# Two stages of a decoder kernel: conv attention with two mix banks, latent attention with two value parts

## The chip, the cores and the metric

One core of a Trainium2 chip runs the kernel. The metric is the device time of one execution in microseconds, as the median over runs.

## The reference

The model is a decoder with two layers. The residual stream x has 4 batches of 1024 rows of 256 numbers. The kernel computes six stages, a to f; the change touches two of them, the conv attention (stage d) and the latent attention (stage e). Cut to these:

```python
def _L1_attn_ref(query, Wq, bq, Wk, bk, Wv, bv, Wo, bo, conv_w, conv_b):   # H = 16 heads of 16
    Q = (query @ Wq.T + bq)...; K = ...; V = ...
    scores = jnp.einsum('bhqd,bhkd->bhqk', Q, K) / np.sqrt(dh)
    # a convolution of width 3 along the keys, over the heads as channels
    x = lax.conv_general_dilated(x, conv_w, window_strides=(1,), padding=[(KS // 2, KS // 2)], ...)
    weights = jax.nn.softmax(x + conv_b, axis=-1)
    out = jnp.einsum('bhqk,bhkd->bqhd', weights, V).reshape(b, s, e)
    return out @ Wo.T + bo

def _L1_xattn_ref(x, latents, mask, ...):                                   # 4 heads of 64
    xn = layernorm(x, ln_x_g, ln_x_b)            # x: the context, 77 rows
    ln = layernorm(latents, ln_l_g, ln_l_b)      # latents: the stream, 1024 rows
    q = ln @ W_q
    kv = jnp.concatenate([xn @ W_kv, ln @ W_kv], axis=1)
    qn = rmsnorm(q, q_gamma) * SCALE; kn = rmsnorm(k, k_gamma)
    sim = jnp.einsum('bhid,bhjd->bhij', qn, kn)  # masked
    attn = jax.nn.softmax(sim, axis=-1)
    out = jnp.einsum('bhij,bhjd->bhid', attn, v)
    return out @ W_out + b_out

x = x + _L1_attn_ref(_layernorm(x), ...)
x = x + _L1_xattn_ref(ctx_1024, _layernorm(x), mask_BxS2_bk0, ...)
```

## The kernel before

Every engine has a program of its own, an instruction list in a fixed order written out by loops in the source; semaphores (`wait_ge`, `then_inc`) tie them together. SP issues the DMAs.

**Conv attention** (`stage_conv_attention`, the span's 860 to 2678 us). The work is 512 units: 4 batches times 16 heads times 8 tiles of 128 query rows. `u` counts them, `b = u // 128`, `at = u % 128`. The score banks are three buffers of two PSUM banks each (banks 0 to 5); banks 6 and 7 are `mix_bank` and `back_bank`. For each unit:
- TensorE, `scores(u)` (L2066): 12 matmuls of 512 columns. It waits for `probs_low` of unit u-3, which frees the buffer.
- VectorE, `maximum(u)` (L2331, L2335), then, in the same turn of its loop, `low_probs(u-1)` (L2340).
- ScalarE, `exps(u)` (L2222), in six of eight units a tap of the key convolution (L2211) or a key half (L2217), then `high_probs(u)` (L2229).
- SP, a DMA transpose of the two halves into `probsT` (L1996). `probsT` has two buffers, one for even and one for odd groups of four units.

For each group of four units: TensorE `mix_values` (L2082: 16 matmuls, each on 32 columns of the array, four side by side), ScalarE `move_mixT` (L2238) from `mix_bank` to `group_mixT`, TensorE `turn_back` (L2092: 4 transposes into `back_bank`), VectorE `normalize` (L2350, L2352, L2355) into `mix`. With `MIX_LAG = 5` the mix of group g stands behind the scores of unit 4g+7, the copy ahead of exps(4g+8), the turn-back behind scores(4g+9), the normalisation at the end of VectorE's turn 4g+10.

The work between batches is spread over the units as "fills", all through `back_bank`: transposes and output products of the batch before (`TURN_FILL`, `OUT_FILL`, units 3 to 16, L2103, L2115), and for the next batch the norm's transposes (`NORM_FILL`, 36 to 48, L2123), query and key columns (`Q_FILL`, `K_FILL`, 52 to 80, L2131) and values (`V_FILL`, 84 to 96, L2138), each at every fourth unit. A fill waits for the normalisation that last read `back_bank`, and the next `turn_back` waits until the fill has been copied out.

**Latent attention** (`stage_latent_attention`, 2678 to 3362 us). First the context's 77 rows are normed and projected (L2598 to L2730). Then for each of four batches: a projection stretch of 14 steps (norm transposes, queries and keys with an RMS norm, their transposes, values), and a score loop of 32 units (4 heads times 8 tiles), taken in pairs. TensorE's order in the loop is scores(2p), scores(2p+1), `project` (L2882), `mix_values` (L2864 to L2873) of earlier pairs. `scores(u)` waits for the exp of unit u-2. The probabilities go exp (L3030), high half (L3037) on ScalarE, low half (L2936) on GpSimd, DMA transpose by SP (L2788) into `probsT`; `halves` and `probs` have three buffers. A value is kept as three bf16 parts: high (ScalarE L3012), left (VectorE L3096), middle (ScalarE L3017), low (GpSimd L2927). A mix multiplies high and middle in one set of 18 matmuls of 128 columns (L2864, L2866), and low in a second set of 18 of 64 columns (L2870, L2873). The norm of the next batch runs inside the loop: `stats` at units 8 to 11, `aggregate` 11 to 14, `rstd_step` on GpSimd 15 to 21, `apply` (L3140) 22 to 29, `add_bias` on GpSimd from 23 on.

## Time and profile before

| | us |
|---|---|
| median of the runs | 3918.76 |
| lowest, highest | 3916.62, 3923.54 |
| the profiled execution | 3912.23 |
| its span | 3910.5 |
| TensorE busy in the span | 3369.3 (86%) |
| VectorE busy | 2928.5 (75%) |
| ScalarE busy | 2601.1 (67%) |
| GpSimd busy | 1826.9 (47%) |
| conv attention, mean DMA share | 0.87 |

Busy times are of one profiled execution. A unit's place in time is read from the timeline, by the start of its first score matmul (two matmuls are merged in one row, "x2"). A row's first two numbers are start and duration in microseconds, those in square brackets the idle time of the engine ahead of it and what ended it.

### The profile page before, as it was taken

The numbers are of one execution on the slowest core, as the hardware profiler recorded it, in microseconds if no ns is written. First come the engines' busy times: TensorE is split into PE (matmuls) and PEld (weight loads), VectorE is DVE, ScalarE is ACT, GpSimd is POOL, SyncE is SP. The second block draws the span as 40 slices with busy tenths as digits, with TensorE's granted clock in tenths as the row PEclk, the third lists the DMA queues.
The fourth block names the chain that finished last, engine by engine and source line by source line (L and its number), as shares of the span: only waits on it lengthen the run. The fifth ranks groups of instructions, "written<-read, shape, count | busy, mean of one in ns | idle before, by whom it ended". The sixth has DMA issues, their size and how long they took to land. (4 is left out here: it accounts for less than half of the span.)

```text
span 3910.5 us, 61085 instructions
## 1 busy us (share of the span) xinstructions
PE 3369.3 (86%) x20113; PEld 2602.9 (67%) x20113; DVE 2928.5 (75%) x5833; ACT 2601.1 (67%) x3897; POOL 1826.9 (47%) x1129
## 2 busy tenths in 40 slices
PE   6867724269999999999999999995889899799999
PEld 4645521147777777777777777773667667699999
DVE  4568789779888888888888889984676666474347
ACT  2334444558888888898888989982667667354443
POOL 0034410016656566565665656642767576360015
PEclk9989956589999999999999999997999999799999
DMA  1047800038889888888888889891749467743224
GB/s 51 0 87 129 147 22 1 1 110 157 151 147 154 147 151 151 146 156 143 154 146 151 155 149 162 162 165 36 124 85 174 80 121 140 204 149 95 76 83 146
DMA packets 1571351, 470.02 MB, mean 120 GB/s; under 512 B 1507174, under 2 KB 1565159, under 8 KB 1569767
## 3 DMA queue, kind: packets, MB, share of 16 engines
q1 hardware_dynamic: 1564903, 449.40, 60.7%
q0 software_dynamic: 6144, 16.79, 1.3%
q8 instruction: 164, 2.69, 0.3%
q14 instruction: 140, 1.15, 0.1%
HBM read 49.00 MB, written 39.58 MB: 23 GB/s over the span
## 5 line engine op out<-in xcount | busy, mean ns | idle before, releaser
L2331 DVE TENSOR_REDUCE d_neg_max<-psum 128x1 f32<-128x1024 f32 x512 | 624.6, 1220 | 161.9 <-PE psum L2066 160.7
L2066 PE MATMUL psum<-d_KH,d_QH 128*128 128x512 f32 x2048 | 685.3, 416 | 25.5 <-DVE d_halves L2340 21.0
L2222 ACT ACTIVATE psum<-psum,d_bias 128x1024 f32<-128x1024 f32 x512 | 558.2, 1090 | 213.9 <-DVE d_bias L2335 203.5
L2340 DVE SCALAR_TENSOR_TENSOR d_halves<-psum,d_halves 128x1024 f16<-128x1024 f32 x512 | 624.3, 1219 | 32.3 <-ACT d_halves L2229 27.7
L2066 PE MATMUL psum<-d_KL,d_QH 128*128 128x512 f32 x2048 | 638.1, 393 | 0.0
L2066 PE MATMUL psum<-d_KH,d_QL 128*128 128x512 f32 x2048 | 636.7, 392 | 0.0
L2022 POOL TENSOR_TENSOR d_KC<-d_KC,d_tap_of 128x1024 f32<-128x1024 f32 x126 | 302.1, 2397 | 536.6 <-ACT d_tap_of L2211 536.6
L2229 ACT ACTIVATE d_halves<-psum 128x1024 f16<-128x1024 f32 x512 | 521.6, 1019 | 3.5
L2066 PEld LDWEIGHTS psum<-d_KH,d_QH 128*128 128x128 f32 x2048 | 356.9, 188 | 173.1 <-issue 68.4
L2066 PEld LDWEIGHTS psum<-d_KL,d_QH 128*128 128x128 f32 x2048 | 384.9, 188 | 87.7
L2066 PEld LDWEIGHTS psum<-d_KH,d_QL 128*128 128x128 f32 x2048 | 384.9, 188 | 87.0
L2029 POOL TENSOR_TENSOR d_KL<-d_KC,d_KH 128x1024 fp32r<-128x1024 f32 x128 | 308.1, 2407 | 112.7 <-ACT d_KH L2217 112.7
L2936 POOL TENSOR_TENSOR e_halves<-e_probs,e_halves 128x1102 f16<-128x1102 f32 x128 | 292.2, 2283 | 122.9 <-ACT e_halves L3037 121.5
L2018 POOL TENSOR_TENSOR d_KC<-d_KC,d_tap_of 128x1024 f32<-128x1024 f32 x126 | 306.8, 2435 | 26.2 <-ACT d_tap_of L2211 17.9
L2211 ACT ACTIVATE d_tap_of<-d_K,d_taps 128x1024 f32<-128x1024 f32 x252 | 288.8, 1146 | 0.0
L3030 ACT ACTIVATE e_probs<-psum,e_neg_max 128x1102 f32<-128x1102 f32 x128 | 150.3, 1174 | 92.9 <-DVE e_neg_max L3109 92.8
L3105 DVE TENSOR_REDUCE e_own_neg_max<-psum 128x1 f32<-128x1102 f32 x128 | 167.1, 1305 | 4.4
L3494 POOL DMA_INDIRECT f_tile<-f_expert_out,f_slots x64 | 60.8, 950 | 231.7 <-DMA f_expert_out<-f_tile 183.8
L3781 DVE TENSOR_TENSOR f_hT_low<-psum,f_hT_high 128x384 fp32r<-128x384 f32 x135 | 75.3, 558 | 117.4 <-ACT f_hT_high L3657 117.2
L3653 ACT ACTIVATE f_silu<-psum 128x352 f32<-128x352 f32 x135 | 62.8, 466 | 145.7 <-PE psum L3543 143.0
L3037 ACT ACTIVATE e_halves<-e_probs 128x1102 f16<-128x1102 f32 x128 | 143.7, 1122 | 23.6 <-DMA e_probsT<-e_halves 20.4
L3657 ACT ACTIVATE f_hT_high<-psum 128x384 fp32r<-128x384 f32 x135 | 66.4, 492 | 137.1 <-PE psum L3563 137.0
(526 smaller groups left out, 7577.7 us busy)
## 6 DMA issues: line engine op xcount, KB each, us to landing
f_weights_raw<-in_L_ffn_packed_dram SPq DMA_DIRECT2D x10, 1088.0 KB, 16.1
f_tile<-expert_rows SPq DMA_DIRECT2D x71, 128.0 KB, 2.2
f_expert_out<-f_tile SPq DMA_DIRECT2D x71, 128.0 KB, 1.7
d_probsT<-d_halves SPq DMA_TRANSPOSE x512, 4.3
f_tile<-f_kept_rows SPq DMA_DIRECT2D x64, 128.0 KB, 2.2
expert_rows<-d_group_mixT SPq DMA_DIRECT2D x7, 1024.0 KB, 11.5
residual_stream<-in_x_dram SPq DMA_DIRECT2D x4, 1024.0 KB, 9.5
f_kept_rows<-residual_stream SPq DMA_DIRECT2D x4, 1024.0 KB, 8.5
```

Of the source, the lines that this page charges most:

```text
L2018: g.tensor_tensor(KC[:, ch, :], KC[:, ch, :], tap_of[:, ch, :], ALU.add)\
L2022: g.tensor_tensor(KC[:, ch, :], KC[:, ch, :], tap_of[:, ch, :], ALU.add)\
L2029: g.tensor_tensor(KL[hh % 2][:, ch, :], KC[:, ch, :], KH[hh % 2][:, ch, :].bitcast(F32), ALU.subtract).then_inc(key_low.sem, 1)
L2066: last = t.matmul(scores_at(u)[:, cols], q_part[:, ch, j * P:(j + 1) * P], k_part[hh % 2][:, ch, cols], start=k == 0, stop=k == 5)
L2211: a.activation(tap_of[:, ch, :], K[b % 2][:, ch, k:S + k], ACT.Copy, scale=taps[:, ch, 3 * h + k:3 * h + k + 1]).then_inc(tapped.sem, 1)
L2222: a.activation(scores_at(u), scores_at(u), ACT.Exp, bias=bias[u % 2][:, 0:1], accum_out=sums[u // 4 % 4][:, u % 4, :]).then_inc(probs_read ...
L2229: a.activation(halves[u % 4][:, 0, :], scores_at(u), ACT.Copy, scale=LIFT)\
L2331: v.tensor_reduce(neg_max[u % 2][:], scores_at(u), AXIS.X, ALU.max, negate=True)\
L2340: v.scalar_tensor_tensor(halves[u % 4][:, 1, :], scores_at(u), LIFT, halves[u % 4][:, 0, :], ALU.mult, ALU.subtract).then_inc(probs_low.se ...
L2936: g.tensor_tensor(halves[i % 3][:, 1, 0:W], probs[i % 3][:], halves[i % 3][:, 0, 0:W], ALU.subtract)\
L3030: a.activation(probs[g % 3][:], scores_at(g), ACT.Exp, bias=neg_max[g % 2][:, 0:1], accum_out=sums[p % 2][:, i:i + 1]).then_inc(probs_read ...
L3105: v.tensor_reduce(own_neg_max[g % 2][:], scores_at(u), AXIS.X, ALU.max, negate=True)\
```

## The change

In the conv attention the mixes of two groups (an even one and the following odd one) stand together behind the scores of unit 8p+11. Even groups use PSUM bank 6, odd groups bank 7, for mix and turn-back both; a mix from group 2 on waits for the normalisation of the group two before. The copies stand ahead of exps 8p+12 (even) and 8p+14 (odd), the turn-backs behind scores 8p+13 and 8p+15, the normalisations in VectorE's turns 8p+14 and 8p+16. The fills get new units and take the bank that `fill_bank` names; turn and out fills alternate by `banks[k // 2]`.

In the latent attention a value is kept as two f16 parts, scaled by a power of two that is worked out from the weights at the stage's start (squares on ScalarE, one matmul, small steps on VectorE, a power on GpSimd); `wo` is scaled back once. The second set of matmuls, the middle copy and GpSimd's low part are gone. The norm's steps stand at other units, and `apply` is another instruction.

```diff
-        mix_bank = PS[:, 6 * BANK:7 * BANK]
-        back_bank = PS[:, 7 * BANK:8 * BANK]
+        banks = [PS[:, 6 * BANK:7 * BANK], PS[:, 7 * BANK:8 * BANK]]
+
+        def fill_bank(at):
+            return banks[0 if at % 8 in (7, 0) else 1]
...
-        TURN_FILL = {3: 0, 4: 1, 7: 2, 8: 3}
-        OUT_FILL = {11: 0, 12: 1, 15: 2, 16: 3}
-        NORM_FILL = {36 + 4 * k: k for k in range(4)}
-        Q_FILL = {52 + 4 * k: k for k in range(4)}
-        K_FILL = {68 + 4 * k: k for k in range(4)}
-        V_FILL = {84 + 4 * k: k for k in range(4)}
-        TAIL = 18
+        PAIRS = GROUPS * B // 2
+        TURN_FILL = {7: 0, 8: 1, 9: 2, 10: 3}
+        OUT_FILL = {15: 0, 16: 1, 17: 2, 18: 3}
+        NORM_FILL = {39: 0, 41: 1, 47: 2, 49: 3}
+        Q_FILL = {55: 0, 57: 1, 63: 2, 65: 3}
+        K_FILL = {71: 0, 73: 1, 79: 2, 81: 3}
+        V_FILL = {87: 0, 89: 1, 95: 2, 97: 3}
+        TAIL = 20
+        MIX_AT, EVEN_MOVED, EVEN_BACK, EVEN_NORM, ODD_MOVED, ODD_BACK, ODD_NORM = 11, 12, 13, 14, 14, 15, 16
...
-                    t.wait_ge(mixT_moved.sem, mixT_moved.at(group))
+                    if group >= 2:
+                        t.wait_ge(normalized.sem, normalized.at(group - 1))
...
+                    pair = pair_at(u, MIX_AT)
+                    if pair is not None:
+                        wait_for_fill(b, at - 3 if at - 3 in FILLS else at - 4)
+                        mix_values(2 * pair)
+                        wait_for_fill(b, at - 1 if at - 1 in FILLS else at - 2)
+                        mix_values(2 * pair + 1)
+                    pair = pair_at(u, EVEN_BACK)
+                    if pair is not None:
+                        turn_back(2 * pair)
+                    pair = pair_at(u, ODD_BACK)
+                    if pair is not None:
+                        turn_back(2 * pair + 1)
+                    if at % 8 in (7, 0):
+                        groups = 2 * ((u - EVEN_BACK) // 8) + 1
+                    else:
+                        groups = 2 * ((u - ODD_BACK) // 8) + 2
...
-        V = sb("V", [P, TB, H, PARTS * HD], BF16)
+        V = sb("V", [P, TB, H, 2 * HD], F16)
...
                     for k in range(TB):
                         for part in range(2):
-                            t.matmul(mix_bank, V[:, k, h, 0:2 * HD], moving(part, k), start=k + part == 0, stop=False)
+                            t.matmul(mix_bank, V[:, k, h, :], moving(part, k), start=k + part == 0, stop=False)
                     for part in range(2):
-                        t.matmul(mix_bank, ctx_values[:, b, h, 0:2 * HD], moving(part, TB)[0:Z, :], start=False,
-                                 stop=False)
-                    for k in range(TB):
-                        for part in range(2):
-                            t.matmul(mix_bank[part * HD:(part + 1) * HD, :], V[:, k, h, 2 * HD:3 * HD],
-                                     moving(part, k), start=False, stop=False)
-                    for part in range(2):
-                        last = t.matmul(mix_bank[part * HD:(part + 1) * HD, :], ctx_values[:, b, h, 2 * HD:3 * HD],
-                                        moving(part, TB)[0:Z, :], start=False, stop=True)
+                        last = t.matmul(mix_bank, ctx_values[:, b, h, :], moving(part, TB)[0:Z, :], start=False,
+                                        stop=part == 1)
...
-                def values_low(b, j):
-                    g.wait_ge(v_middle.sem, v_middle.at(TB * b + j + 1))
-                    g.tensor_tensor(V[:, j, :, 2 * HD:3 * HD], left[j % 2][:], V[:, j, :, HD:2 * HD], ALU.subtract)\
-                        .then_inc(v_low.sem, 1)
...
-                        if b + 1 < B and 15 <= u < 22:
-                            rstd_step(b + 1, u - 15)
-                        if b + 1 < B and 23 <= u < 23 + TB:
-                            add_bias(TB * (b + 1) + u - 23)
+                        if b + 1 < B and 9 <= u < 16:
+                            rstd_step(b + 1, u - 9)
+                        if b + 1 < B and 22 <= u < 22 + TB:
+                            add_bias(TB * (b + 1) + u - 22)
...
-                def value_left(b, j):
+                def value_low(b, j):
                     v.wait_ge(v_high.sem, v_high.at(TB * b + j + 1))
-                    v.wait_ge(v_low.sem, v_low.at(TB * b + j - 1))
-                    v.tensor_tensor(left[j % 2][:], bank(j % 2)[:, 0:D].rearrange("p (h e) -> p h e", h=H),
-                                    V[:, j, :, 0:HD], ALU.subtract).then_inc(v_left.sem, 1)
+                    v.scalar_tensor_tensor(V[:, j, :, HD:2 * HD],
+                                           bank(j % 2)[:, 0:D].rearrange("p (h e) -> p h e", h=H), v_scale[:, 0:1],
+                                           V[:, j, :, 0:HD], ALU.mult, ALU.subtract).then_inc(v_low.sem, 1)
...
-                    v.tensor_scalar(n.xn[:, tile, :], X[:, TB * b + tile, :], n.mv[:, tile, 0:1],
-                                    n.rstd[:, tile:tile + 1], ALU.subtract, ALU.mult).then_inc(n.normed.sem, 1)
+                    v.scalar_tensor_tensor(n.xn[:, tile, :], X[:, TB * b + tile, :], n.mv[:, tile, 0:1],
+                                           n.rstd[:, tile:tile + 1].to_broadcast([P, D]), ALU.subtract, ALU.mult)\
+                        .then_inc(n.normed.sem, 1)
...
-                        if b + 1 < B and 8 <= u < 12:
-                            stats(b + 1, 2 * u - 16)
-                            stats(b + 1, 2 * u - 15)
-                        if b + 1 < B and 11 <= u < 15:
-                            aggregate(b + 1, 2 * u - 22)
-                            aggregate(b + 1, 2 * u - 21)
+                        if b + 1 < B and 3 <= u < 7:
+                            stats(b + 1, 2 * u - 6)
+                            stats(b + 1, 2 * u - 5)
+                        if b + 1 < B and 6 <= u < 10:
+                            aggregate(b + 1, 2 * u - 12)
+                            aggregate(b + 1, 2 * u - 11)
```

## Rows read from the trace of the kernel before

**Rows 1.** Windows: stretch, its us, busy us of each engine, PEclk, DMA share, GB/s

```profile
875.00:2645.00 1770.00, 1730.35 (x9043) 1286.35 (x9041) 1547.72 (x2067) 1555.14 (x2106) 1072.07 (x524) 1.00 0.87 152
3265.00:3340.00 75.00, 73.80 (x584) 60.04 (x583) 47.66 (x101) 56.18 (x81) 52.84 (x24) 1.00 1.03 176
```

**Rows 2.** Timeline of TensorE, conv stage, from unit 152 to unit 160

```profile
1401.26 0.74 PE L2066 MATMUL psum<-d_KH,d_QH 128*128 128x512 f32 x2
...
1406.90 0.60 PE L2092 MATMUL psum<-ident,d_group_mixT 128*128 128x128 f32 x4
1407.26 0.71 PE L2066 MATMUL psum<-d_KH,d_QH 128*128 128x512 f32 x2
...
1427.38 0.73 PE L2066 MATMUL psum<-d_KH,d_QH 128*128 128x512 f32 x2
```

**Rows 3.** Timeline of TensorE around one mix

```profile
1453.55 0.62 PE L2066 MATMUL psum<-d_KL,d_QH 128*128 128x512 f32 x2
1454.01 0.63 PE L2066 MATMUL psum<-d_KH,d_QL 128*128 128x512 f32 x2
1454.56 1.05 PE L2082 MATMUL psum<-d_probsT,d_V 128*32 128x512 f16 x16
1455.54 0.74 PE L2066 MATMUL psum<-d_KH,d_QH 128*128 128x512 f32 x2
1456.12 0.63 PE L2066 MATMUL psum<-d_KL,d_QH 128*128 128x512 f32 x2
```

**Rows 4.** Timeline of VectorE and ScalarE, unit 152 and the next maximum

```profile
1404.34 1.23 DVE L2331 TENSOR_REDUCE d_neg_max<-psum 128x1 f32<-128x1024 f32 x1 [0.42 <-PE psum L2066]
...
1405.91 1.09 ACT L2222 ACTIVATE psum<-psum,d_bias 128x1024 f32<-128x1024 f32 x1 [0.34 <-DVE d_bias L2335]
...
1407.10 1.22 DVE L2331 TENSOR_REDUCE d_neg_max<-psum 128x1 f32<-128x1024 f32 x1
1408.06 1.01 ACT L2229 ACTIVATE d_halves<-psum 128x1024 f16<-128x1024 f32 x1
...
1409.11 1.23 DVE L2340 SCALAR_TENSOR_TENSOR d_halves<-psum,d_halves 128x1024 f16<-128x1024 f32 x1 [0.47 <-ACT d_halves L2229]
```

**Rows 5.** Timeline, a normalisation and the turn fill that waits for it

```profile
1324.80 0.68 DVE L2350 TENSOR_REDUCE d_group_sum<-psum 128x64 f32<-128x512 f32 x1
...
1325.94 0.42 PEld L2103 LDWEIGHTS psum<-ident,d_mix 128*128 128x128 f32 x4 [0.49 <-DVE d_mix L2355]
```

**Rows 6.** Timeline of TensorE, a column fill and one octet, unit 181 to 189

```profile
1499.64 1.88 PE L2131 MATMUL psum<-d_ln_xT,d_wq 128*128 128x512 f32 x4
1500.95 1.03 PE L2066 MATMUL psum<-d_KH,d_QH 128*128 128x512 f32 x2
...
1529.69 1.03 PE L2066 MATMUL psum<-d_KH,d_QH 128*128 128x512 f32 x2
```

**Rows 7.** Timeline of TensorE, latent stage, one mix and the scores behind it

```profile
3288.44 1.91 PE L2864 MATMUL psum<-e_probsT,e_V 128*128 128x256 f16 x16
...
3290.50 1.06 PE L2870 MATMUL psum<-e_probsT,e_V 128*64 128x256 f16 x16
...
3291.61 0.50 PE L2845 MATMUL psum<-e_KH,e_QS 128*128 128x512 f32 x1
```

**Rows 8.** Timeline of TensorE, the scores seven pairs later

```profile
3337.95 0.50 PE L2845 MATMUL psum<-e_KH,e_QS 128*128 128x512 f32 x1
```

**Rows 9.** Page, DMA issues: operation, count, median us to landing

```profile
e_probsT<-e_halves SPq DMA_TRANSPOSE x128, 4.8
```

**Rows 10.** Page, groups: busy us, mean ns, idle before

```profile
L2936 POOL TENSOR_TENSOR e_halves<-e_probs,e_halves 128x1102 f16<-128x1102 f32 x128 | 292.2, 2283 | 122.9 <-ACT e_halves L3037 121.5
L3037 ACT ACTIVATE e_halves<-e_probs 128x1102 f16<-128x1102 f32 x128 | 143.7, 1122 | 23.6 <-DMA e_probsT<-e_halves 20.4
```

**Rows 11.** By line: duration ns min/median/max, first and last start

```profile
L3140 DVE TENSOR_SCALAR e_ln_xn<-residual_stream,e_ln_mean_var,e_ln_rstd x24: 406/946/2032, 2836.8 to 3180.8; 128x256 f32<-128x256 f32 x24
...
L2368 DVE TENSOR_TENSOR d_QL<-d_ln_xn,d_QH x32: 411/418/2496, 859.7 to 2223.3; 128x256 fp32r<-128x256 f32 x32
```

More of the change, by code:

```diff
@@ L2081, in mix_values @@
                             part, tile = lane % 2, k + lane // 2
-                            last = t.matmul(mix_bank[lane * 32:(lane + 1) * 32, :], V[:, side, tile, h, :],
+                            last = t.matmul(banks[group % 2][lane * 32:(lane + 1) * 32, :], V[:, side, tile, h, :],
                                             probsT[group % 2][:, part * TB + tile, :, :]
@@ L2087, in turn_back @@
                 def turn_back(group):
-                    if group:
-                        t.wait_ge(normalized.sem, normalized.at(group))
                     t.wait_ge(mixT_moved.sem, mixT_moved.at(group + 1))
                     for k in range(4):
-                        last = t.transpose(back_bank[:, k * P:(k + 1) * P], group_mixT[:, k * P:(k + 1) * P],
+                        last = t.transpose(banks[group % 2][:, k * P:(k + 1) * P], group_mixT[:, k * P:(k + 1) * P],
                                            core.ident[:])
@@ L2100, in turn_mix @@
                         t.wait_ge(mixT_ready.sem, mixT_ready.at(4 * b + k))
+                    bank = banks[k // 2]
                     for i in range(2):
                         for ch in range(DC):
-                            last = t.transpose(back_bank[:, (ch * 2 + i) * P:(ch * 2 + i + 1) * P],
+                            last = t.transpose(bank[:, (ch * 2 + i) * P:(ch * 2 + i + 1) * P],
                                                mix[:, 2 * k + i, ch * P:(ch + 1) * P], core.ident[:])
@@ L2292, in _ @@
                     b, at, hh, j = u // U, u % U, u // TB, u % TB
-                    if u >= MIX_LAG + 3 and (u - MIX_LAG - 3) % 4 == 0 and (u - MIX_LAG - 3) // 4 < GROUPS * B:
-                        move_mixT((u - MIX_LAG - 3) // 4)
+                    pair = pair_at(u, EVEN_MOVED)
+                    if pair is not None:
+                        move_mixT(2 * pair)
+                    pair = pair_at(u, ODD_MOVED)
+                    if pair is not None:
+                        move_mixT(2 * pair + 1)
                     if u < ALL:
@@ L2520, in stage_latent_attention @@
     KB = WP // P
-    PARTS = 3
+    V_REACH = float(1 << 15)
     TILES = TB * B
@@ L2687, in _ @@
                 def _(t):
+                    t.wait_ge(v_squares_done.sem, v_squares_done.at(3))
+                    t.matmul(PS[:, 6 * BANK:6 * BANK + 3], core.ones[:], v_squares[:], start=True, stop=True)\
+                        .then_inc(v_totalled.sem, 1)
                     t.wait_ge(ctx_vec.sem, ctx_vec.at(3 * B))
```

184 lines of the change are left out of this document (110 added, 74 removed).

## The prediction

> **Which views, in which order.** First the busy table of stretches [rows 1], to be read by stage: a change in one stage is worth what that stage's last wait gives. In the conv stage TensorE is busy 1730 of 1770 us, VectorE 1548 and ScalarE 1555: three engines near their limit. In the latent stage's score loop TensorE is busy 73.8 of 75 us, and the DMA engines show a share of 1.03. Neither stage has an engine whose relief alone shortens it much. Then the timelines, to see which wait ends last.
>
> **Conv stage, a stretch without fills.** Eight units take 26.1 us, from 1401.26 to 1427.38 [rows 2]. I name the units of an octet 0 to 7. TensorE's own work in it: a score unit is 12 matmuls of 0.23 (two of them step by 0.46, [rows 3]), so 2.75. The first unit behind a mix is 2.87, because the next pair of matmuls comes after 0.58 and not 0.46. A mix is 0.98, entered 0.09 late, at 1454.56 and not 1454.47. A turn-back is 0.36 [rows 2]. For eight units: 22.2 + 2 x 1.07 + 2 x 0.36 = 25.0. So 1.1 us of every octet is waiting: scores(u) needs low_probs(u-3).
>
> One unit on the other engines [rows 4]: its maximum starts 2.96 to 3.08 after its scores do; exp follows 1.57 after the start of the maximum; the high half starts 2.15 after exp when a tap stands between and takes 1.01; the low half takes 1.23. VectorE's step from one maximum to the next is 2.76, and a normalisation adds 1.0 (one starts at 1324.80 and the TensorE that waits for it is freed at 1325.94, 1.1 later [rows 5]). So VectorE needs 8 x 2.76 + 2 x 1.0 = 24.1.
>
> Walking the old order by hand with these durations (mixes behind units 3 and 7, copies before exp of 0 and 4, turn-backs behind 1 and 5, normalisations in 2 and 6) settles at 26.1 in the second octet: the row's value. That is why I trust the walk to some tenths.
>
> **The new order, same walk.** Two mixes stand behind unit 3. TensorE saves one exit and one entry: 0.12 + 0.09 + about 0.1 = 0.3 per octet, 64 octets, 20 us if TensorE sets the pace. But the burst is 0.1 + 0.98 + 0.86 = 1.93, and VectorE sits idle 1.4 us before unit 4's maximum. From the start of unit 3's scores to unit 6's maximum TensorE leads: 2.75 + 1.93 + 2.87 + 2.75 + 0.36 + 2.96 = 13.6. From there VectorE leads until the low half of the next unit 0, which unit 3 needs: four steps of 2.76, the two normalisations (now in iterations 6 and 0, so both inside this stretch) 2.0, and 0.2 of waiting for ScalarE: 13.2. Sum 26.8, against 26.1: +0.75 per octet. Some 30 of the 64 octets are without fills: **+23 us** (bounds 0 and +40).
>
> Beside the first rule of this walk: the Trainium skill (TensorEngine Tiling (Array Packing), Key Properties) says that changing the tiling mode drains TensorE. By that rule alone, fewer changes of mode mean a shorter stage, which is the rival 'Drained less' below. The trace agrees that a change costs: 0.09 at the entry [rows 3].
>
> **Octets with fills.** In the octets with query, key and value columns TensorE really is the bound: 28.74 us [rows 6], 25.0 + 2 x 1.31 for the columns + 2 x 0.4 by which the scores behind them are longer = 28.4. There 0.3 comes off. But a fill now stands one unit behind the normalisation that frees its bank (iteration 6 for the fill behind unit 7, iteration 0 for that behind unit 1); before it was two. The old turn_mix(0) stands one unit behind too, and there TensorE waits 0.49 even with a mix of 0.98 in between [rows 5]. A fill has no mix in between. By the walk: VectorE ends the normalisation 3.9 after unit 6's maximum starts, TensorE arrives 0.95 earlier; at the second fill 1.2 earlier. So +2.15 of waiting, less 0.3 and less the 0.2 of old slack: +1.7. There are 6 such octets in each of three batches: 18 x 1.7 = **+30 us** (bounds +8 and +45). In the 6 octets with norm transposes the wait that leaves (turn_back had to wait for the fill's copy in the one shared bank) is as large as the new one: 0. The turn and out fills save about 2 us, since two banks alternate; the tail has both turn-backs behind the last transposes, +2. SP's transposes of an even group now wait for a mix that ends some 4 us later; they catch up, since at a share of 0.87 one is 3.0 us of DMA time in a unit of 3.45 [rows 1], and the high half that reuses the buffer comes 4 us later still: 0. If that cover were gone, ScalarE would wait for the transposes once per octet, and behind it exp of the next unit. The wait for the normalisation that mix_values now carries is met by an operation of the octet before: 0.
>
> Conv stage: +23 + 30 + 0 = **+53 us**.
>
> **Latent stage.** A pair of units: 18 matmuls of 128 columns from 3288.44, 18 of 64 columns from 3290.50, the next scores at 3291.61 [rows 7]. The second set goes: 1.11 + 0.1 for its entry = 1.2 us of TensorE per pair. The mean pair takes (3337.95 - 3291.61)/7 = 6.62 [rows 7, 8]. TensorE would then need some 5.3: it stops being the bound, and the whole 1.2 can't be had. What is late next:
> - the score loop: scores(u) need exp(u-2). My estimate from the loop's unit times, scores 1.35, mask and maximum 1.85, exp, high half and next exp 3.6, with the overlap of two units, gives 5.5 per pair.
> - the DMA queue: at share 1.03 a transpose costs 1.03 x 3.31 = 3.4 us of 16 engines. I take 1.15 as the share it can reach: 2.95 each, 5.9 per pair.
> - the three buffers of halves: high half 1.12, low half 2.28 [rows 10], transpose 4.8 to landing [rows 9], some 0.2 between: 8.4 us, and nearer 9 with two transposes in flight. Three units per 9 us is 6.0 per pair.
>
> I take 6.0: 0.6 per pair on 44 pairs = 26 us. In the last four pairs of the first three batches the apply of the next norm holds VectorE: 0.95 us median, 0.41 at best [rows 11]. The change writes it as scalar_tensor_tensor with two SBUF tensors. That form's nearest row is the conv stage's QL, also two SBUF tensors: 0.41 at best, 2.50 where a GpSimd operation runs [rows 11]. So the new apply waits for GpSimd as the old one, and these 12 pairs gain 0.2: 2 us. The first mix of a batch stands on the path: 1.1 x 4 = 4. In the stretch between batches the last three mixes and the value steps lose 3.5 each time: 10. (Two of the three mixes are on the path there, 2.4; the rest is that a value bank comes free after two steps and not behind ScalarE's middle copy and GpSimd's low part, which go too.) The tail: 3. At the stage's start three squares on ScalarE, one matmul, seven small VectorE steps and one pow on GpSimd are new, and the pow stands ahead of the next norm's chain; one split of the context's values goes from VectorE's path. I bound this between -1 and +3 and take 0. The statistics (units 3 to 6) and the rstd steps on GpSimd (9 to 15, between its low halves) move ahead; VectorE's are hidden where it waits for the first mix, GpSimd's are the same work in another place: 0, and 2 us if the two pows now delay a transpose that was not late before. Sum **-46 us** (bounds -20 and -75).
>
> The Trainium skill (SBUF — State Buffer, Who interferes with whom) says that a VectorE instruction with two SBUF inputs contends with a GpSimd instruction that reads SBUF. It speaks against the new apply, and the 2.50 us row agrees.
>
> **Sum.** +53 - 46 = +7 us. The profiled execution took 3912.23 (span 3910.5), 6.5 below the median of the runs, 3918.76; so 3919 in the profile's terms, and **3926** as a median. 0.2% of this kernel, 8 us, is about what a measurement can tell from no change.
>
> **Rivals.**
> - *Drained less* (0.2). TensorE is the bound all over the conv stage, normalisations come in time, and the stage gives the 20 us of the 64 saved entries and exits. For it: 97.8% busy [rows 1]. Against it: the 1.1 us per octet of waits. 3918.8 - 20 - 46 = 3853.
> - *Latent at its compute limit* (0.22). The DMA queue carries 5.5 per pair: 44 x 1.15 = 51 rather than 26: 3901 to 3907. For it: DMA share is not shown to be a limit. Against it: 1.03 already. This is the case on the other side of mine; it decides from a share of 3.41 x 2 / 5.5 = 1.24 up.
> - *Held by the transposes* (0.24). The pair stays near 6.4, latency growing as the queue fills: 10 us from the pairs and -29 in all; with the bound of +30 for the no-fill octets: 3943 to 3955.
> - *Forecast* (0.34): 3911 to 3941.
> - That the third part of the values is not removed is excluded by the diff.
>
> **Chances.** Below 3911: all of the first, most of the second (0.16), 0.04 of the forecast: 0.40. Within 8 us: 0.17. Above: 0.43. Cases of both signs are likely, the forecast's own range is 3911 to 3941. The range for 8 in 10 runs from 3862, which leaves out half of the first rival, to 3956.
>
> **What would show it.** Right: fill-free octets near 26.8, the scores of units 1 and 3 waiting for d_halves; column octets near 30.4, with a wait for d_mix of about 1 us before L2131's matmuls; pairs near 6.0 with DMA share about 1.15; the apply still near 1 us. Wrong: octets at 25.8 and 28.4, or pairs at 5.5.

## The result, and the profile of the changed kernel

The changed kernel takes 3987.69 us in the median (3983.34 to 3992.21), the kernel before 3921.15 (3916.62 to 3927.30) beside it: a ratio of 1.0167, 95% interval 1.0148 to 1.0185. Forecast was 3926, with a range up to 3956. The profiled executions have spans of 3985.2 and 3910.5. Read by stage, from the first instruction of one stage to the first of the next:

| stage | before | after | difference | forecast |
|---|---|---|---|---|
| ahead of the conv attention | 830.0 | 833.2 | +3 | 0 |
| conv attention | 1848.2 | 1947.6 | **+99** | +53 |
| latent attention | 688.7 | 661.6 | **-27** | -46 |
| behind it | 543.6 | 542.8 | -1 | 0 |

Both stages moved the way that was forecast, and both missed its size to the slower side. A stage's length differs between profiles of one and the same code: the latent stage of before took 685.3 to 693.1 us in eight profiles (before and seven experiments), that of after 661.6 to 666.1 in three. The windows of the two stages (stretch, its us, busy us of each engine, PEclk, DMA share, GB/s) answer to [rows 1]:

```profile
885.00:2745.00 1860.00, 1730.16 (x9028) 1297.90 (x9028) 1555.52 (x2059) 1549.05 (x2099) 1061.74 (x522) 1.00 0.81 145
3345.00:3420.00 75.00, 65.17 (x398) 52.94 (x396) 50.79 (x107) 58.55 (x85) 54.24 (x24) 0.98 1.03 179
```

In the conv stage the engines do the same work (TensorE 1730 busy in both) in 1860 us and not 1770: TensorE fell from 97.8% to 93% busy. What came in is waiting. In the latent stage TensorE has 65 us of work in 75 where it had 74, and the DMA share is 1.03 as before.

What TensorE waited for in the conv stage (engine, line, releaser: us in total, times, longest), first before:

```profile
PE psum L2066 <- DVE d_halves L2340: 21.0, 38, 2.2
PE psum L2092 <- ACT d_ln_xT L2245: 5.7, 12, 1.0
PE psum L2115 <- DVE d_mix L2355: 2.3, 6, 0.6
```

and after:

```profile
PE psum L2073 <- DVE d_halves L2368: 56.2, 75, 2.4
PE psum L2139 <- DVE d_mix L2383: 27.1, 24, 1.4
PE psum L2131 <- DVE d_mix L2383: 13.8, 12, 1.3
PE psum L2146 <- DVE d_mix L2383: 13.0, 12, 1.1
PE psum L2123 <- DVE d_mix L2383: 9.4, 6, 2.0
```

63 us of waits of fills for a normalisation (`d_mix`), and 35 us more of scores waiting for the low half three units back. A fill-free octet of the last batch, TensorE's timeline (start, us), from one burst of two mixes to the next:

```profile
2593.45 1.91 PE L2090 MATMUL psum<-d_probsT,d_V 128*32 128x512 f16 x32
...
2611.17 0.73 PE L2073 MATMUL psum<-d_KH,d_QH 128*128 128x512 f32 x2 [0.71 <-DVE d_halves L2368]
2617.33 0.73 PE L2073 MATMUL psum<-d_KH,d_QH 128*128 128x512 f32 x2 [0.38 <-DVE d_halves L2368]
2620.28 1.91 PE L2090 MATMUL psum<-d_probsT,d_V 128*32 128x512 f16 x32
```

2620.28 - 2593.45 = 26.83. The walk gave 26.8, with the scores of units 1 and 3 waiting for d_halves: so it is. Its two stretches, read from the starts and ends in the timeline, are 13.8 (from unit 3's scores to unit 6's maximum; forecast 13.6) and 13.0 (from there to the end of the low half of the next unit 0; forecast 13.2). An octet with query columns:

```profile
1534.63 1.91 PE L2090 MATMUL psum<-d_probsT,d_V 128*32 128x512 f16 x32
...
1549.93 1.98 PE L2139 MATMUL psum<-d_ln_xT,d_wq 128*128 128x512 f32 x4 [1.29 <-DVE d_mix L2383]
...
1558.44 1.98 PE L2139 MATMUL psum<-d_ln_xT,d_wq 128*128 128x512 f32 x4 [1.01 <-DVE d_mix L2383]
...
1565.86 1.91 PE L2090 MATMUL psum<-d_probsT,d_V 128*32 128x512 f16 x32
```

31.2 us (28.74 before [rows 6]; forecast 30.4). VectorE and GpSimd around the first of the two waits:

```profile
1548.10 0.68 DVE L2378 TENSOR_REDUCE d_group_sum<-psum 128x64 f32<-128x512 f32 x1
1548.97 0.90 DVE L2383 TENSOR_TENSOR d_mix<-d_group_sum,d_inv_sum 128x64 f32<-128x64 f32 x1
```

```profile
1548.52 1.27 POOL L2054 TENSOR_TENSOR residual_stream<-residual_stream,d_bo 128x512 f32<-128x512 f32 x1
```

L2383 takes 0.22 to 0.24 alone; here 0.90, and it ends 0.08 behind GpSimd's addition. The same instruction of the same octets is as long in before (0.91), where two units lie between it and the fill. TensorE pays for that now, since it stands behind this normalisation.

The 63 whole octets of the stage, each from the start of unit 4's maximum to that of the next octet's, after less before, by what stands in them (sums over the batches, worked out from the starts of the 512 maxima in either timeline; an apply is the last step of a norm on one tile, a split takes the low part of the queries, both on VectorE):

| octets | count | difference, us | forecast |
|---|---|---|---|
| none of what follows | 27 | +21 | 27 x 0.75 = +20 |
| columns and values | 18 | +43.5 | +30 |
| applies of the next norm (units 28 to 36) | 3 | +7.0 | counted with the first row, +2.3 |
| splits of the next queries (units 124 to 132) | 3 | +6.0 | counted with the first row, +2.3 |
| norm transposes | 6 | +4.9 | 0 |
| turn and out fills | 6 | +14.2 | -2 |
| beginning and tail | | +3 | +2 |

Of the last row's 3 us, 2.2 lie ahead of the first maximum, where the profiles read 41.7 to 44.0 in no order of the kernels; the tail gives 0.8.

The latent stage: its four score loops take 393.3 us, from the first maximum of each to its last, before 412.9; the three gaps between loops 164.5 (170.0); from the last maximum to the next stage 23.5 (25.5); the beginning 80.3 (80.2). Mix and scores of a pair, to [rows 7]:

```profile
3374.31 1.91 PE L2937 MATMUL psum<-e_probsT,e_V 128*128 128x256 f16 x16
...
3376.19 0.48 PE L2920 MATMUL psum<-e_KH,e_QS 128*128 128x512 f32 x1
...
3380.58 1.91 PE L2937 MATMUL psum<-e_probsT,e_V 128*128 128x256 f16 x16 [0.21 <-issue]
...
3387.91 1.91 PE L2937 MATMUL psum<-e_probsT,e_V 128*128 128x256 f16 x16
```

1.88 from mix to scores where it was 3.17; pairs of 6.27 and 7.33. ScalarE's high half (page, groups) and the apply (by line: min/median/max ns), to [rows 10, 11]:

```profile
L3092 ACT ACTIVATE e_halves<-e_probs 128x1102 f16<-128x1102 f32 x128 | 143.6, 1122 | 44.3 <-DMA e_probsT<-e_halves 41.3
```

```profile
L3194 DVE SCALAR_TENSOR_TENSOR e_ln_xn<-residual_stream,e_ln_mean_var,e_ln_rstd x24: 481/1164/2398, 2932.6 to 3264.7; 128x256 f32<-128x256 f32 x24
```

The wait for transposes went from 20.4 to 41.3 us, and the new apply is slower than the old one (1164 against 946).

### The profile page after: what moved, and what is told of

Same layout as the page of the kernel before. It is cut to its first block and busy times, and to the rows that moved or that the text cites. A ratio compares the mean times of both kernels' runs of the same rounds, so it can differ in the third digit from the quotient of the medians.

```text
span 3985.2 us, 58619 instructions
## 1 busy us (share of the span) xinstructions
PE 3306.3 (83%) x18960; PEld 2565.5 (64%) x18963; DVE 2947.1 (74%) x5839; ACT 2592.4 (65%) x3871; POOL 1799.0 (45%) x1098
## 5 line engine op out<-in xcount | busy, mean ns | idle before, releaser
L2073 PEld LDWEIGHTS psum<-d_KH,d_QH 128*128 128x128 f32 x2048 | 365.0, 189 | 202.7 <-DVE d_halves L2368 74.7
L3092 ACT ACTIVATE e_halves<-e_probs 128x1102 f16<-128x1102 f32 x128 | 143.6, 1122 | 44.3 <-DMA e_probsT<-e_halves 41.3
```

Of the source, the lines that this page charges most:

```text
L2073: last = t.matmul(scores_at(u)[:, cols], q_part[:, ch, j * P:(j + 1) * P], k_part[hh % 2][:, ch, cols], start=k == 0, stop=k == 5)
```

## The experiments

Times are medians; each ratio is to the kernel before, run beside it. Line numbers in the rows are those of each run's own kernel.

**Each half alone.** e1 has the conv attention of after and the latent attention of before; e2 the other way round.

```diff
 e1:  stage_conv_attention of after, stage_latent_attention of before
 e2:  stage_conv_attention of before, stage_latent_attention of after
```

> The conv attention of after, the latent attention of before. In the profile of after the conv stage starts at 833 and the latent stage at 2781, 1948 us, against 830 to 2678, 1848 us, in before: +99. If the stages are independent this kernel is at 3921 + 99 = 4020, between 4012 and 4028, slower than after. If the conv change also shifts something in the latent stage (clock, queue of transposes), it is off this by more than 8 us.

> The conv attention of before, the latent attention of after. The latent stage of after takes 661.6 us to the first work of the next stage, before 688.7: -27. Independent stages: 3921 - 27 = 3894, between 3887 and 3901. The forecast's term was -46, which would be 3875.

e1: 4013.72, ratio 1.0232 (1.0214 to 1.0250). e2: 3903.21, ratio 0.9935 (0.9916 to 0.9954). In the profiles the conv stage takes 1944.5 in e1, the latent stage 666.1 in e2. 1.0232 x 0.9935 = 1.0165, the ratio of the whole change within its interval: the two halves don't meet. By the medians they are +91 and -20, by the ratios +91 and -25. e2 lies just above its expected 3887 to 3901.

**Fills one unit later.**

```diff
-        NORM_FILL = {39: 0, 41: 1, 47: 2, 49: 3}
+        NORM_FILL = {40: 0, 42: 1, 48: 2, 50: 3}
 (Q_FILL, K_FILL, V_FILL alike)
```

> e1 with the norm, query, key and value fills one unit later (behind units 0 and 2 of an octet, not 7 and 1). Theory 'the fill waits for the normalisation': TensorE's waits for d_mix ahead of L2131, L2139 and L2146 (54 us in after) go nearly to zero, of the 2.4 us that a column octet lost some 1.5 to 2 come back, and the stage is 25 to 40 us shorter than in e1. Rival 'the wait only moves': the paired mixes behind unit 3 now wait for the copy of the fill behind unit 2, by 1 to 2 us per octet, and the stage is within 10 us of e1. Rival 'the burst of two mixes is the cost': the octets stay at 31.

3972.33, ratio 1.0133 (1.0110 to 1.0155); the stage is 1903.7, 41 less than in e1. One octet with query columns and one with key columns:

```profile
1540.25 2.04 PE L2090 MATMUL psum<-d_probsT,d_V 128*32 128x512 f16 x32
1557.23 1.88 PE L2139 MATMUL psum<-d_ln_xT,d_wq 128*128 128x512 f32 x4
1564.62 1.98 PE L2139 MATMUL psum<-d_ln_xT,d_wq 128*128 128x512 f32 x4
1567.20 0.73 PE L2073 MATMUL psum<-d_KH,d_QH 128*128 128x512 f32 x2 [0.59 <-DVE d_halves L2368]
1570.16 2.06 PE L2090 MATMUL psum<-d_probsT,d_V 128*32 128x512 f16 x32
...
1598.96 1.91 PE L2090 MATMUL psum<-d_probsT,d_V 128*32 128x512 f16 x32
1615.80 1.88 PE L2139 MATMUL psum<-d_ln_xT,d_wk 128*128 128x512 f32 x4
1623.02 1.88 PE L2139 MATMUL psum<-d_ln_xT,d_wk 128*128 128x512 f32 x4
1627.60 1.91 PE L2090 MATMUL psum<-d_probsT,d_V 128*32 128x512 f16 x32
```

No fill waits for d_mix, and the mixes behind unit 3 don't wait for the copy either: the first theory holds, the two others fall. With key columns an octet is 28.64, and before it was 28.73: TensorE has no idle time in it, and the switches saved give 0.1, not 0.3. With query columns it is 29.91, 1.2 above before, and the scores wait for the low half (0.59). With values it is 29.75 to 29.79 in five octets and 28.64 in one, the octet from 92 to 100 of the first batch. VectorE copies queries and values and not keys, but the copies aren't the difference: that one octet has the same four copies of 0.41 as its neighbour from 84 to 92. What differs is the second normalisation. Here it is in the octet from 84 to 92 (29.77 us), VectorE and GpSimd, and then in that from 92 to 100:

```profile
1186.02 2.33 DVE L2383 TENSOR_TENSOR d_mix<-d_group_sum,d_inv_sum 128x64 f32<-128x64 f32 x1
```

```profile
1185.87 2.41 POOL L2029 TENSOR_TENSOR d_KC<-d_KC,d_tap_of 128x1024 f32<-128x1024 f32 x1 [4.02 <-ACT d_tap_of L2235]
```

```profile
1215.78 0.22 DVE L2383 TENSOR_TENSOR d_mix<-d_group_sum,d_inv_sum 128x64 f32<-128x64 f32 x1
```

Started 0.15 behind GpSimd's instruction it lasts until that one ends; in the octet of 28.64 it starts 0.14 ahead of it and takes 0.22. All six octets with queries have it at 1.98 to 2.34, none of those with keys has. Of the 43.5 us some 32 go with the fills' later place (the 18 octets of e3 against those of e1); the 12 that are left stand in the 11 octets with the held normalisation.

**Two banks without the pairing.** Banks alternate, but each group's mix, copy, turn-back and normalisation stand where before had them, and so do the fills.

```diff
-        MIX_AT, EVEN_MOVED, EVEN_BACK, EVEN_NORM, ODD_MOVED, ODD_BACK, ODD_NORM = 11, 12, 13, 14, 14, 15, 16
+        EVEN_MIX, EVEN_MOVED, EVEN_BACK, EVEN_NORM = 7, 8, 9, 10
+        ODD_MIX, ODD_MOVED, ODD_BACK, ODD_NORM = 11, 12, 13, 14
-            return banks[0 if at % 8 in (7, 0) else 1]
+            return banks[0 if at % 8 in (3, 4) else 1]
+ (fills at the units of before)
```

> The conv attention with two banks as in after, even groups in bank 6 and odd groups in bank 7, but the mixes not paired: mix, copy, turn-back and normalisation of each group stand where before had them, and so do the fills, each in the bank that has just been normalised. The latent attention of before. Theory 'pairing is the cost, not the two banks': fill-free octets at 26.0 (26.85 in after), column octets at 28.7, no wait for d_mix at the fills, and turn_back no longer waits for a fill's copy (7 us in before): 3905 to 3921 in all. Rival 'alternating banks itself costs' (group_mixT has still one buffer, the mix waits for the normalisation of the group two before): octets of 26.8 and over, 3940 and more.

3914.25, ratio 0.9970 (0.9954 to 0.9986), 99 us below e1. The mixes of a fill-free octet at the same place as above:

```profile
2589.29 1.05 PE L2091 MATMUL psum<-d_probsT,d_V 128*32 128x512 f16 x16
2593.50 0.74 PE L2074 MATMUL psum<-d_KH,d_QH 128*128 128x512 f32 x2 [0.21 <-DVE d_halves L2371]
2602.43 1.05 PE L2091 MATMUL psum<-d_probsT,d_V 128*32 128x512 f16 x16
2615.22 1.05 PE L2091 MATMUL psum<-d_probsT,d_V 128*32 128x512 f16 x16
```

25.93 and not 26.83; column octets are at 28.73. The pairing is the whole cost, the held instructions included: from the first maximum to the last, e4 is 1.8 us shorter than before. The second bank alone is worth a little: the octets with norm transposes are 27.0 and 26.9 (28.1 and 27.4 before), since turn_back no longer waits for the fill's copy.

**Output products spread.**

```diff
-        OUT_FILL = {15: 0, 16: 1, 17: 2, 18: 3}
+        OUT_FILL = {16: 0, 24: 1, 26: 2, 34: 3}
-        TAIL = 20
+        TAIL = 36
```

> e3 with the four output products of the batch before behind units 16, 24, 26 and 34 (in e3 15 to 18). In e3 the octet from unit 12 to 20 takes 37.2 (31.15 in before), with waits for d_mix of 1.1 and 1.98 ahead of L2123 and, in after, a granted clock of 0.66 behind the second. Theory 'these waits and the clock behind them': no wait for d_mix ahead of L2123, the octets from 12 to 36 together 26.3 + 37.2 + 29.2 = 92.7 in e3 become 83 to 87, so 18 to 28 us less than e3. Rival 'the products themselves': each octet gets 1.5 per product and the sum is within 1.5 us of e3's.

3968.07, ratio 1.0118 (1.0094 to 1.0141). The three octets from 12 to 36 take 89.3, 90.9 and 87.2 in the batches that have products, in e3 91.2, 92.8 and 91.0: 2 to 4 less, where I expected 6 to 10. No product waits for d_mix any more, but each adds its 1.54 to a paired octet in full (27.1 + 26.3 + 29.2 + 4 x 1.54 = 88.8): the rival was the larger half. What the waits cost in after shows here, TensorE's timeline, the normalisation that it waited for, and the windows:

```profile
1411.07 2.51 PE L2123 MATMUL psum<-d_wo,d_K 128*128 128x256 f32 x8 [1.98 <-DVE d_mix L2383]
1413.02 1.41 PE L2073 MATMUL psum<-d_KH,d_QH 128*128 128x512 f32 x2
```

```profile
1409.03 1.98 DVE L2383 TENSOR_TENSOR d_mix<-d_group_sum,d_inv_sum 128x64 f32<-128x64 f32 x1 [0.46 <-DVE d_inv_sum L2380]
```

```profile
1404.00:1409.00 5.00, 5.00 (x23) 3.93 (x21) 3.91 (x6) 2.80 (x4) 0.41 (x1) 1.00 0.60 113
1411.00:1416.00 5.00, 4.93 (x15) 4.00 (x16) 3.24 (x5) 3.16 (x4) 2.15 (x2) 0.66 0.01 3
```

L2383 takes 1.98 here (2.34 in the two later batches) and not 0.22, beside a GpSimd instruction of 2.34 that started at 1408.59: 1.76 of the 1.98 us of TensorE's second wait are this hold. TensorE stood for 1.98 us, and behind it the granted clock is 0.66: the lower of its two levels, 1.2 GHz, for (1 - 0.66)/0.5 = 0.68 of these 5 us. The same pair of scores, which takes 1.41 at 1413.02, took 0.82 at 1405.97, behind the product before.

**What an octet is made of.** e6 makes the burst shorter, e7 the normalisation; both are from e1 and leave work out.

```diff
 e6:
-                    for k in range(0, TB, 2):
+                    for k in range(0, TB // 2 if group % 2 else TB, 2):
 e7:
-                    v.tensor_reduce(group_sum[:], parts, AXIS.X, ALU.add)
+                    v.tensor_reduce(group_sum[:, 0:1, :], parts[:, 0:1, :, :], AXIS.X, ALU.add)
```

> e1 with half of the matmuls of the odd group's mix left out (8 of 16; the output of the conv attention is then not the reference's): the burst of two mixes is 0.43 us shorter, VectorE has the same work. Theory 'an octet is a stretch led by TensorE, the burst in it, and then a stretch led by VectorE': a fill-free octet falls from 26.85 by about 0.4. Rival 'VectorE or ScalarE alone sets the octet': it stays at 26.85.

> e1 with the sum of a normalisation over a quarter of its columns (the output of the conv attention is then not the reference's): VectorE saves about 0.4 in each of two normalisations per octet, TensorE has the same work. By the same theory a fill-free octet falls from 26.85 by about 0.8, to 26.0 to 26.1, and the wait for d_mix ahead of the column fills by 0.4 each, so that a column octet falls from 31.1 to about 30.3. Rival 'TensorE's burst is all of it': 26.85 stays.

3983.78 and 3964.20, one run each. Bursts in the same octet of e6, then of e7:

```profile
2592.66 1.48 PE L2091 MATMUL psum<-d_probsT,d_V 128*32 128x512 f16 x24
2619.07 1.48 PE L2091 MATMUL psum<-d_probsT,d_V 128*32 128x512 f16 x24
```

```profile
2592.30 1.91 PE L2090 MATMUL psum<-d_probsT,d_V 128*32 128x512 f16 x32
2615.37 0.74 PE L2073 MATMUL psum<-d_KH,d_QH 128*128 128x512 f32 x2 [0.17 <-DVE d_halves L2369]
2618.34 1.91 PE L2090 MATMUL psum<-d_probsT,d_V 128*32 128x512 f16 x32
```

26.41 and 26.04. 0.43 us off TensorE's burst gives 0.42, all of it in the first stretch (13.8 to 13.4). In e7 the second stretch goes from 13.0 to 12.2 and the first stays. VectorE's two sums are 0.8 shorter (0.68 to 0.28 each); the first L2383 of the octet, which GpSimd held for 0.76, is down to 0.22 besides, so VectorE has 1.33 less to do and the octet gives 0.79. A new wait of the low half for ScalarE (0.26) takes a part of the rest. No single engine sets this octet: it is a stretch led by TensorE followed by one led by VectorE, as in the walk. The column octets of e7 fell to 30.8 (queries, beside GpSimd's additions) and 29.75 (keys, values); I expected 30.3.

**VectorE's other work.** From e1, the applies of the conv stage's next norm in other turns.

```diff
-                    if b + 1 < B and 27 <= at < 27 + TB:
-                        apply(b + 1, at - 27)
+                    if b + 1 < B and at in (27, 35, 43, 44):
+                        (two applies)
```

> e1 with the eight applies of the conv stage's next norm not one in each of VectorE's turns 27 to 34 but two in each of the turns 27, 35, 43 and 44, where VectorE then waits for the scores behind the burst of two mixes. The octet from 28 to 36 is 29.24 in e1 (26.92 in before). Theory 'work of VectorE costs its whole time in the stretch that VectorE leads and little ahead of the burst's end': that octet falls to 26.9 to 27.3, and the next one (28.57), whose turn 43 is ahead of the burst's end and turn 44 behind it, rises by no more than 0.8. Rival 'the work itself has to be paid anywhere': the two octets together keep their 57.8.

4015.60, one run. The octet from 28 to 36 fell to 26.84 in all three batches (29.24, 32.00 and 29.26 in e1); six applies in turns 27, 35 and 43 cost nothing. The two in turn 44 cost 1.7 (the octet from 44 to 52: 30.3, before the move 28.56), where I allowed 0.8. VectorE, and GpSimd beside it:

```profile
1505.18 2.00 DVE L2452 TENSOR_SCALAR d_ln_xn<-residual_stream,d_ln_mean_var,d_ln_rstd 128x256 f32<-128x256 f32 x2
```

```profile
1504.32 2.39 POOL L2036 TENSOR_TENSOR d_KL<-d_KC,d_KH 128x1024 fp32r<-128x1024 f32 x1
```

Two applies of 0.4 each took 2.0: the first 1.68, until 0.15 behind the end of GpSimd's instruction, the second 0.40. The rival falls for six of the eight. Turn 44 lies in a third octet, which the expectation left out; the three together go from 86.4 to 85.7 only. The experiment doesn't part two causes: the six applies that cost nothing took 0.40 each, while in after those of turns 28 and 33 took 1.68 and 1.10 (0.60 and 0.60 in before), so a turn without room and a turn beside GpSimd's instruction are the same turns here. What a hold alone costs shows in the second batch of e1, where the apply of turn 30 took 2.62 and the octet 32.0 and not 29.25, and in the third batch of e4 (2.64, and 30.5 and not 26.9).

**The latent attention.** From here every kernel has the conv attention of e4.

> The conv attention of e4 and the latent attention of after. Apart they gave 3914 and 3903 against 3923. Independent: 3923 - 9 - 20 to -25 = 3889 to 3895, faster than before by 0.7 to 0.9%.

e8: 3886.39, ratio 0.9910 (0.9892 to 0.9927), faster than either kernel and 3 us below the expected 3889 to 3895. Its latent stage takes 662.9. Then three edits of it, and one (e12) that leaves work out:

```diff
 e9 (apply as before):
-                    v.scalar_tensor_tensor(n.xn[:, tile, :], X[...], n.mv[:, tile, 0:1], n.rstd[...].to_broadcast([P, D]), ...)
+                    v.tensor_scalar(n.xn[:, tile, :], X[...], n.mv[:, tile, 0:1], n.rstd[:, tile:tile + 1], ...)
 e10 (four buffers):
-        halves = [sb(f"halves{i}", [P, 2, WP], F16) for i in range(3)]
+        halves = [sb(f"halves{i}", [P, 2, WP], F16) for i in range(4)]
 e11 (norm steps at before's units):
-                        if b + 1 < B and 9 <= u < 16:
+                        if b + 1 < B and 15 <= u < 22:
 (statistics, aggregates and bias additions alike)
 e12 (half of each transpose; the mix reads the high half in the place of the low one):
-                    sp.dma_start_transpose(probsT[p % 2][:, :, i, :], halves[g % 3][:].rearrange("p a s -> p (a s)"))
+                    sp.dma_start_transpose(probsT[p % 2][:, 0:KB, i, :], halves[g % 3][:, 0, :])
```

> e8 with the apply of the next norm written as before (TENSOR_SCALAR). In after the new form takes 1164 ns in the median (481 at best), the old one took 946 (406). In the last four pairs of a batch an apply that waits for GpSimd's low half holds the mask and the maximum behind it: 6.79 per pair with the new form. Theory 'the form of the instruction': 12 pairs get 0.1 to 0.4 shorter, 1 to 5 us in all. Rival 'any apply there waits for GpSimd as long': pairs at 6.7 to 6.8, no change that can be measured.

> e8 with four buffers of halves in the latent attention, not three. The high half then waits for the transpose four units back. Theory of the forecast's third bullet, 'three buffers of halves hold the pair at 6.0': pairs 3 to 10 of a batch, 6.1 in the mean in e2, fall to 5.5 to 5.7, some 20 us in all. Rival 'the queue of transposes': share at 1.04 to 1.06 already, transposes land later, pairs stay at 6.0 to 6.2 and nothing is gained.

> e8 with statistics, aggregates, rstd steps and bias additions of the next norm at the units that before had. Theory 'the move is worth nothing': within 3 us of e8. Rival: the rstd steps between units 15 and 21 and the aggregates at 11 to 14 stand in front of low halves and maxima that TensorE now waits for, 3 to 8 us more than e8.

> e8 with only the high half of the probabilities transposed in the latent attention, and the mix reading it in place of the low half too (the output is then not the reference's): half of the transposes' bytes, all other work the same. It shows what the other engines allow. Theory 'the transposes hold the pair': the DMA share falls to near 0.5, pairs 3 to 10 go to 5.1 to 5.5 and the whole is 25 to 35 us below e8. Rival 'the other engines are at their limit': pairs stay near 6.0.

> e8 with both the old form of apply and four buffers of halves. The forecast took the pair to be held by the three buffers and the queue; e10 gave 0.2 per pair and e9 0.3 on 12 pairs. If these add: e8 3886 - 6 - 4 = 3876, between 3870 and 3882. If one bound hides the other, it stays at 3880 to 3884.

| | us | ratio, interval | latent stage | mean pair 3 to 10 | mean pair with applies |
|---|---|---|---|---|---|
| before | | | 688.7 | 6.68 | 6.81 |
| after | 3987.69 | 1.0167 | 661.6 | 6.21 | 6.90 |
| e8 | 3886.39 | 0.9910 (0.9892 to 0.9927) | 662.9 | 6.25 | 7.00 |
| e9 | 3880.37 | 0.9900 (0.9876 to 0.9924) | 655.2 | 6.26 | 6.71 |
| e10 | 3882.66 | 0.9898 (0.9874 to 0.9922) | 661.1 | 6.05 | 6.79 |
| e11 | 3890.69 | 0.9925 (0.9901 to 0.9949) | 670.7 | 6.29 | 7.76 |
| e12 | 3862.21 | one run | 628.8 | 5.81 | 6.84 |
| e13 | 3879.58 | 0.9878 (0.9861 to 0.9894) | 652.8 | 6.06 | 6.66 |

The pairs are means over the batches of the step from one even unit's maximum to the next. In time e8 to e11 can't be told from each other, their intervals overlap, and stages of one code differ by up to 8 us between profiles. So e10's stage is that of e8, and e9's 7.6 us less are no proof. e9: the pairs with applies are 0.3 shorter with the old form (and 0.1 in e13 against e10), and its 24 applies take 26.8 us of VectorE and not 31.8; but in the code of before such pairs read 6.81 to 7.30 from profile to profile, so that the form is the cause is likely and not shown. e11: 7.76 in these pairs lies outside the 6.90 to 7.01 of after, e2 and e8; the steps moved up were worth some 8 us with the new apply: the rival was right and my 0 to 2 wrong. e12: the transposes hold the loop, the DMA share falls from 1.04 to 0.64 (windows of e8, then e12) and the stage by 34 us; but pairs 3 to 10 only to 5.8, not 5.1 to 5.5, and 12 us come from the pair that holds the first mix (9.95 to 6.93, four times). In time it is 24 us below e8, 25 to 35 were expected. The granted clock goes from 0.94 to 1.00 in these windows, so a part of the gain can be TensorE's own speed; the run doesn't part them.

```profile
3230.00:3305.00 75.00, 65.78 (x398) 53.47 (x398) 48.47 (x101) 56.73 (x82) 53.25 (x24) 0.94 1.04 183
```

```profile
3230.00:3285.00 55.00, 51.63 (x327) 43.17 (x326) 40.85 (x88) 47.45 (x69) 44.97 (x20) 1.00 0.64 104
```

e10 tells which part of the transposes it is. In its view of what the high half waits for there is no entry for the transposes; in e8's stands

```profile
  DMA e_probsT<-e_halves: 37.8, 39
```

so that wait went with the fourth buffer, and the pair shortened by 0.2 only (share 1.08). The mix waits for the same transposes instead: in pairs 3 to 10 it starts within 0.1 us of the landing of its second transpose in all 32 cases, in e8 in 20 of 32, and in e12 in 5 (worked out from landings and starts in the traces). SP issues 51 of the 64 transposes of these pairs straight behind the one before, and an issue takes it 2.9 us of the 3.2 from one to the next (1.3 in e12): the queue is the bound, the buffers are not. e13, with e9's and e10's edits together, has the shortest latent stage (652.8), the best ratio of those that do all the work, and 3879.58 us, inside the expected 3870 to 3882; with these intervals it can't be told from e9, nor whether the two edits add.

## Why the prediction was wrong

**Right.** The walk: 26.8 was forecast for a fill-free octet and 26.83 measured, and its stretches are 13.8 and 13.0 for 13.6 and 13.2, two errors of 0.2 that cancel; e6 and e7 move them one by one. The mechanism in the column octets: the fill waits for the normalisation one unit too soon (e3), for 2.2 to 2.3 us per octet where 2.15 was forecast. That a saved mode switch would not pay for the pairing: the rule of the Trainium skill (TensorEngine Tiling (Array Packing), Key Properties), that a change of mode drains TensorE, agrees with the rows, yet in e3's key octets, where TensorE is the bound, all of it is 0.1 of 28.7 us. 'Drained less' is excluded by e1.

**Wrong, the conv stage: +99 and not +53.** Four steps.
- "The turn and out fills save about 2 us": +14.2, the largest miss, -2.3 in the octets with turns and +16.6 in those with products. The four products stand behind units 15 to 18, all in one octet; I looked at their bank and not at the normalisations that they wait for: 1.1 and 1.98 in each batch, and 1.6 of slow clock in two of three. The 1.98 is a normalisation that GpSimd held to 1.98 and 2.34, where I had costed one at 1.0 with its sums. Spreading the products gave 2 to 4 per batch (e5), 8 us in all; that the rest is the products in a full octet is worked out from e5's sum alone.
- The column octets: 43.5 and not 30. The waits are 40.1 (27.1 in 12 octets, 13.0 in 6), forecast 38.7. What failed are the two credits set against them, 0.3 for the switch and 0.2 for old slack, 9 us in all: the switch gave 0.1 (e3), and before has no idle time of TensorE in these octets. Some 3 to 5 us are open. VectorE's copies are not it: octets with queries lost 2.55, with keys, which ScalarE copies, 2.35, with values 2.35.
- "Some 30 of the 64 octets are without fills." Six of these hold other work of VectorE, seven applies or the splits of queries, costed at nothing: +2.3 and +2.0 each, not 0.75. I had shown that VectorE leads half the octet. It also isn't the same work: with the pairing an apply of each batch takes 1.68 and another 1.10 (0.60 each in before), a split 2.43 and another 1.21 (0.43 each), all to 0.15 to 0.28 behind the end of an instruction of GpSimd. e14 shows that the applies are the cost; how much of it is the hold and how much the missing room stays open, and for the splits nothing was tried.
- The norm octets: +4.9 and not 0. The wait that left (5.7 us in all) is smaller than the one that came (13.8), lengthened by GpSimd's addition of the bias (0.90 for 0.24).

Behind the first and third is one step that the walk didn't take: VectorE's instructions were walked at the length that they have alone, or had in before, though the regrouping changes which of them start beside one of GpSimd's. One smaller reading is off too: the sum of TensorE's own work in an octet gave 25.0 and so 1.1 of waiting, where the timeline of before has TensorE idle for 0 to 0.2 in octets of 25.9.

**Wrong, the latent stage: -27 and not -46.** The terms as listed add up to 45. The term of the pairs: I took 0.6 off each of 44, from a pair of 6.62 that would go to 6.0; 0.4 came off in the mean (6.68 to 6.21 in pairs 3 to 10, 6.71 to 6.43 in the last four of the last batch, 5.0 to 4.8 in the first two), 18 us and not 26. I had chosen the largest of three bounds, the buffers at 6.0; e10 shows that the queue holds even without them, so its share of 1.15, which I took without a row for it, was too high: 1.03 to 1.08 is what it reaches. The applies: +1 and not -2. The rule of the Trainium skill (SBUF — State Buffer, Who interferes with whom) and its row, quoted for this, spoke against the new form, and the trace agrees (1164 ns in the median against 946); it should have set the term and not only a warning. But the old form, with one SBUF tensor, is held as well, up to 2.03 us. The gaps: -5.5 and not -10. First mixes -3 (forecast -4), tail -2 (-3), beginning 0 (0); the first mixes differ by as much between profiles of one code.

**The range.** All four conv terms missed to one side, and my bounds were for terms that miss apart. The bounds that I gave (+40 and +45 in the conv stage, -20 in the latent) add up to 3984, near the 3988 that came; the range stopped at 3956, 32 us short. Even the rival 'held by the transposes' was priced too low by these: 3943 with +40 in the place of +23 is 3960, not 3955.

## What to carry to other kernels

Putting two short operations together saves their switch and makes one long gap for the engine that feeds on them; that engine then leads the rest of the period. Other work of it costs nothing where the gap stands (six applies in e14) and much behind it (up to 1.7 for two). Count its other work per period before costing any of it at nothing, and look which of its instructions will now start beside a long one of GpSimd: such a start made 2.3 us out of 0.2 here. Ask of each fill not which buffer it uses but which instruction frees that buffer, and how long ago. Try the second buffer and the regrouping apart: the one gave 0.3% (e4), the other took 2.6% (e1 against e4).

## What the runs showed of the hardware

- VectorE's instructions with two SBUF operands that start beside one of GpSimd's last until that one's end: 0.22 became 2.33 beside 2.41 (e3), and an apply of 0.48 took up to 2.40 in after. Started 0.14 ahead of GpSimd's instruction, the same one took its 0.22, and GpSimd its 2.41. TENSOR_SCALAR with one SBUF tensor is held too: 1.68 instead of 0.40 (e14), and 2.62 in e1 though it started 0.09 ahead of GpSimd's. The held ones end 0.07 to 0.28 behind GpSimd's.
- The clock falls after a stop of 1.98 us, but not each time: in the same octet of e3, behind the same 1.98, the next scores took 0.82, at full clock.

```profile
1391.20 1.99 PE L2123 MATMUL psum<-d_wo,d_K 128*128 128x256 f32 x8 [1.98 <-DVE d_mix L2383]
1392.85 0.82 PE L2073 MATMUL psum<-d_KH,d_QH 128*128 128x512 f32 x2
```

  Such octets are 35.6, those with the slow clock 37.2. What decides is open; it wasn't tried.
- Stages that no kernel here touches differ by several us between profiles: the time ahead of the conv stage from 823.9 to 835.7, the stage behind the latent one from 539.4 to 547.5, and the latent stage of before, in kernels that left it alone, from 685.3 to 693.1. Octets of one kind agree to some 0.05 us, apart from those in which a VectorE instruction was held, and told 0.1 us apart where whole times could not tell 6.
